# Rebuilding the first stage of a ternary-weight FFN kernel on one Trainium2 core: indices on VectorE, maxima over partitions on TensorE, another order of loads and masks

## The reference, cut to what matters

```python
w = weights[conditions]                        # 128 batches choose among 200 matrices of 64 x 64
c = jnp.einsum('bct,bcd->bdt', x, w)           # x: 128 x 64 x 512, fp32

def ternarize(W, threshold):                   # threshold 0.05
    absW = jnp.abs(W)
    delta = threshold * jnp.max(absW)
    mask = absW > delta
    n = jnp.maximum(jnp.sum(mask), 1)
    alpha = jnp.sum(jnp.where(mask, absW, 0.0)) / n
    return alpha * jnp.sign(W) * mask

h = gelu(c @ ternarize(W1).T + b1)             # W1: 2048 x 512
y = h @ ternarize(W2).T + b2                   # W2: 512 x 2048
scale = jnp.max(jnp.abs(y)) / 7 + 1e-8         # over all of y
out = x + clip(round(y / scale), -7, 7) * scale
```

## Time and profile before

| what | us |
|---|---|
| median of 3 runs | 1045.27 (1043.31 to 1045.33) |
| the profiled execution, its own time | 1043.61 |
| its span, first to last instruction | 1041.8 |
| PE busy in the span | 937.6 |
| DVE / ACT / POOL busy | 648.8 / 553.8 / 157.8 |

### The profile page before, as it was taken

The page is one execution under the profiler, slowest core; times in us unless marked ns, Lnnn a source line. Parts: engine busy times, 40 slices in busy tenths (PEclk is TensorE's granted clock), DMA queues, the critical chain, the costliest instruction groups (busy, mean ns, idle before and its releaser), DMA issues.

```text
span 1041.8 us, 15013 instructions
## 1 busy us (share of the span) xinstructions
PE 937.6 (90%) x5265; PEld 448.1 (43%) x5265; DVE 648.8 (62%) x1007; ACT 553.8 (53%) x710; POOL 157.8 (15%) x213
## 2 busy tenths in 40 slices
PE   0499999999999999999999999999999999999600
PEld 0355444444444444444444444444444444444200
DVE  3599766666666656666665666566666656633492
ACT  3489372727456473828274564638282645535290
POOL 4032303030110203030302102030303021000000
PEclk9899999999999999999999999999999999999855
DMA  6610120301121211203011112121030121105999
GB/s 219 201 44 4 30 63 11 70 21 40 45 45 41 50 40 43 48 10 78 13 40 45 45 40 50 40 50 41 10 81 10 40 47 44 40 0 181 307 386 376
DMA packets 40592, 77.89 MB, mean 75 GB/s; under 512 B 3952, under 2 KB 4352, under 8 KB 40064
## 3 DMA queue, kind: packets, MB, share of 16 engines
q1 hardware_dynamic: 36304, 73.47, 24.3%
q0 software_dynamic: 4096, 3.94, 1.4%
q10 hardware_dynamic: 176, 0.27, 0.1%
HBM read 60.89 MB, written 16.78 MB: 75 GB/s over the span
## 4 chain that ended last, share of the span: by engine, by line
PE 77%; issue 10%; ACT 5%; DVE 3%; POOL 2%; DMA 1%; DVEq 0%; ACTq 0%; SPq 0%; POOLq 0%
PE ps L444 38%; PE ps L456 35%; PE ps L432 3%; ACT y L692 2%; PE ps L474 1%; ACT y L664 1%; POOL ws L356 1%; DVE st L709 1%; DMA yx<-in_x 1%; DVE y L822 0%; DVE y L960 0%; ACT ps L692 0%; DVE wts L819 0%; DMA condb<-in_itok_B 0%; DVE st L768 0%
## 5 line engine op out<-in xcount | busy, mean ns | idle before, releaser
L444 PE MATMUL ps<-yc,wts 128*128 128x512 f16 x2048 | 447.3, 379 | 0.3 <-ACT g L596 0.3
L456 PE MATMUL ps<-wts 128*128 128x512 f16 x1920 | 419.3, 379 | 0.7 <-ACT wts L620 0.7
L444 PEld LDWEIGHTS ps<-yc,wts 128*128 128x128 f16 x2048 | 199.4, 98 | 238.7 <-ACT g L596 0.8
L456 PEld LDWEIGHTS ps<-wts 128*128 128x128 f16 x1920 | 185.8, 98 | 220.4 <-ACT wts L620 0.9
L742 DVE SCALAR_TENSOR_TENSOR wts<-g,st,wts 128x512 f16<-128x512 f32 x256 | 186.4, 749 | 143.0 <-ACT wts L601 141.1
L596 ACT ACTIVATE g<-ps,b1t,st 128x512 f32<-128x512 f32 x256 | 197.8, 773 | 116.7 <-PE ps L444 109.3
L601 ACT ACTIVATE wts<-g,st 128x512 f16<-128x512 f32 x256 | 181.0, 713 | 0.0
L583 ACT ACTIVATE xs<-yx,st 128x2048 f16<-128x2048 f32 x28 | 56.1, 2002 | 145.0 <-DVE st L777 145.0
L378 POOL PARTITION_ALL_REDUCE st<-st x46 | 21.5, 467 | 669.1 <-DVE st L711 413.6
L356 POOL DMA_INDIRECT wg<-in_L_cond_weights,ids x112 | 106.5, 951 | 41.3 <-issue 29.3
L747 DVE SCALAR_TENSOR_TENSOR y<-ps,st,b2b 128x512 f32 (+1 forms) x56 | 41.9, 748 | 78.0 <-PE ps L456 78.0
(11 more groups left out here) (118 smaller groups left out, 377.2 us busy)
## 6 DMA issues: line engine op xcount, KB each, us to landing
yx<-in_x SPq DMA_DIRECT2D x56, 512.0 KB, 6.1
out<-wts SPq DMA_DIRECT2D x12, 512.0 KB, 10.2
y<-in_x SPq DMA_DIRECT2D x5, 1024.0 KB, 10.0
wts<-in_x SPq DMA_DIRECT2D x10, 512.0 KB, 6.0
y<-in_L_ffn_W SPq DMA_DIRECT2D x8, 512.0 KB, 9.0
wts<-in_x SPq DMA_DIRECT2D x4, 1024.0 KB, 5.6
y<-in_L_ffn_W SPq DMA_DIRECT2D x4, 1024.0 KB, 8.0
out<-y SPq DMA_DIRECT2D x4, 1024.0 KB, 12.5
```

The lines of the kernel that those rows point to most:

```text
L444: last = nc.tensor.matmul(psH[:, j % HB, :], T1T[:, k, j * P:(j + 1) * P], csp[:, a, k, :], start=(k == 0 and a == 0), stop=(k == KT - 1 a ...
L456: last = nc.tensor.matmul(psY[:, r % 2, :], hsp[:, a, j, r * P:(r + 1) * P], T2T[:, j, :], start=(j == 0 and a == 0), stop=(j == HT - 1 an ...
```

## The change

Part by part:

- **Indices and constants.** DVE makes the indices (a scan of ones gives 0 to 127, a 32 x 32 transpose brings them to partitions) and the identity matrices; POOL's iota, elementwise instructions and `affine_select` are gone. `condb` is loaded on ACT's queue and `b2b` behind the |W1|.
- **Direct conditioning.** Batches go to two sides of 64 partitions, so a gather fills 128 partitions with two matrices: 4 gathers for a block in place of 8, and no cleared diagonal. The product is `condition_direct`: 16 matmuls of 64 x 128 by 64 x 64 for a half in place of 8 of 128 x 128 by 128 x 128. `x` of blocks 0 and 1 is loaded as four DMAs of 64 partitions (`load_direct`).
- **Maxima by PE.** `wide` spreads a column over 128 columns on DVE, `all_partitions` transposes it on PE in fp32, and DVE reduces the result along the row: for the maximum of `W1`, of the gathered matrices and of `x` of block 0. The scale of `c` of block 0 now comes from the bound 128 x max|x| x max|w| in place of the maximum of `c`, so it is known before `c` is: `high_c0` and `low_c0` read `c` straight from PSUM. POOL's reduction is kept for `b1` (`b1max_all`), behind the gathers of block 0 and ahead of those of block 1.
- **Masks and turns.** All four masks of `W1` stand ahead of its signs, which are cut into 8 pieces; 3 turns in place of 6 stand ahead of `first(0, 0)`, and the tables `AFTER` and `STORES` set where the others go. Two stores follow each gelu at j = 8 to 13 in place of 10 to 15.
- **Loads.** SP issues `W1`, `x` of block 0 and `W2` with no wait between; the half of `x` of block 2 waits for `wide_used`.
- **The count of W2** is PE's: `count2`, 32 matmuls of 512 columns between the last turn of `W2` and `second(0, 0)`, read by DVE after its first `aw2` instruction. It uses the bank `psN`, one of the two banks of `c`, so the conditioning of block 1 stands one `second` later for both halves. ACT's four instructions are gone.

```diff
+    AHEAD, EARLY = 3, 6
+    AFTER = {0: [(1, 3)], 1: [(1, 4)], 2: [(1, 5)], 3: [(1, 6), (1, 7)], **{j: [(1, j + 4)] for j in range(4, 12)}}
+    for j, more in {8: (0,), 9: (1,), 10: (2, 3), 11: (4,), 12: (5, 6), 13: (7, 8), 14: (9, 10), 15: (11,)}.items():
+        AFTER[j] = AFTER.get(j, []) + [(2, n) for n in more]
+    TURNED = 12
+    ORDER = [(1, j) for j in range(AHEAD)] + [piece for j in range(HT) for piece in AFTER[j]] \
+        + [(2, j) for j in range(TURNED, HT)]
+    STORES = [1] * 8 + [2] * 6 + [1] * 2
...
-            sp.dma_start(condb[:, :], cond.rearrange("(a b) -> a b", a=1).to_broadcast([P, B])).then_inc(cond_loaded, 16)
             for c in range(LOADS):
                 sp.dma_start(w1s[:, c * HL:(c + 1) * HL, :], W1_v[:, c * HL:(c + 1) * HL, :]).then_inc(w1_loaded[c], 16)
-            load_direct(0)
-            sp.wait_ge(w_gathered[1], 16 * HALF)
+            load_direct(0, (0, 1))
             for n in range(RT):
                 sp.dma_start(w2s[:, n, :], W2_v[:, n, :]).then_inc(w2_loaded[n], 16)
+            sp.wait_ge(wide_used, 1)
             load_half(0, DIRECT * BB)
-            sp.wait_ge(t1_made, WCH)
+            sp.wait_ge(t1_made, HT // MASKED)
             sp.wait_ge(w1abs_made, LOADS)
-            load_direct(1)
+            load_direct(1, (0, 1))
...
+            def gather_direct(b):
+                for r in range(RT):
+                    nc.gpsimd.indirect_dma_start(
+                        out=wdirect[:, b, r, :], out_offset=None, in_=w_rows[:, :],
+                        in_offset=bass.IndirectOffsetOnAxis(ap=idsd[:, b, r:r + 1], axis=0)).then_inc(wd_gathered[b], 16)
+
+            pool.wait_ge(idx_made, 1)
+            gather_direct(0)
...
-            all_max(max1_part, 1, mx1r, mx1, max1_all)
-            all_max_c(0)
+                all_max(cmax_part, b, mr, ms, cmax_all)
+
+            all_max(b1max_part, 1, mx1r[:, 1:2], mx1[:, 1:2], b1max_all)
...
+            def condition_direct(b, half, bank):
+
+                for k in range(KT):
+                    for j in range(2):
+                        for s in range(2):
+                            side = slice(s * C, (s + 1) * C)
+                            last = nc.tensor.matmul(bank[:, s, k, j * C:(j + 1) * C],
+                                                    xdirect[b][side, 2 * half + j, k * P:(k + 1) * P],
+                                                    wdirect[side, b, 2 * half + j, :], start=True, stop=True)
+                last.then_inc(c_made, 1)
+
+            def all_partitions(q, wide):
+                nc.tensor.transpose(psM[:, q, :], wide, idf).then_inc(wide_turned, 1)
...
+            def count2():
+
+                pe.wait_ge(t2_made, WCH)
+                for n in range(RT):
+                    for c in range(WCH):
+                        hc = slice(c * T, (c + 1) * T)
+                        nc.tensor.matmul(psN, ones[:, :], tern2[:, n, hc], start=(n == 0 and c == 0), stop=False)
+                        last = nc.tensor.matmul(psN, twos[:, :], neg2[:, n, hc], start=False,
+                                                stop=(n == RT - 1 and c == WCH - 1))
+                last.then_inc(n2_counted, 1)
...
-            nc.tensor.transpose(psY[:, 0, 0:HT], b1r[:, :], idf[:, :]).then_inc(b1_turned, 1)
-            condition(0, 0, direct=True)
-            condition(0, 1, direct=True)
-
+            nc.tensor.transpose(psY[:, 0, 0:HT], b1r[:, :], idf[0:HT, 0:HT]).then_inc(b1_turned, 1)
+            pe.wait_ge(wide_made, 1)
+            all_partitions(2, wide1)
             pe.wait_ge(b1_ready, 1)
-            pe.wait_ge(c_copied, 1)
             count1(0)
             count1(1)
-            for j in range(HC):
-                turn1(j)
+            pe.wait_ge(wide_made, 2)
+            all_partitions(1, wide_w)
+            pe.wait_ge(wide_made, 3)
+            all_partitions(0, wide_x)
+            pe.wait_ge(xdirect_loaded, 64)
+            pe.wait_ge(wd_gathered[0], 16 * RT)
+            condition_direct(0, 0, psCd0)
+            condition_direct(0, 1, psCd1)
             count1(2)
             count1(3)
-            for j in range(HC, AHEAD):
+            pe.wait_ge(wide_used, 1)
+            for j in range(AHEAD):
                 turn1(j)
-            pe.wait_ge(c_copied, 2)
+            pe.wait_ge(c0_split, 4)
...
-            condition(1, 0, direct=True)
+                pe.wait_ge(w_stored, ORDER.index((1, j)) + 1)
+                first(0, j, wait_bank=j >= HB, wait_c=False)
+                for weight, n in AFTER[j]:
+                    turn1(n) if weight == 1 else turn2(n)
             for j in range(TURNED, HT):
                 turn2(j)
+            pe.wait_ge(n_read, 1)
+            count2()
             pe.wait_ge(w_stored, 2 * HT)
...
-                condition(i + 1, 1, direct=first_block)
+                if first_block:
+                    pe.wait_ge(xdirect_loaded, 128)
+                    pe.wait_ge(wd_gathered[1], 16 * RT)
+                    pe.wait_ge(n2_read, 1)
+                    condition_direct(1, 0, psCd)
+                else:
+                    condition(i + 1, 1)
                 second(i, 1, wait_bank=not first_block)
+                if first_block:
+                    pe.wait_ge(c_copied, 1)
+                    condition_direct(1, 1, psCd)
...
+            def low_c0(half, s, bank):
+                dve.wait_ge(c0_hi_made, 2 * half + s + 1)
+                nc.vector.scalar_tensor_tensor(out=rows_of_side(csp[:, 1, :, :], half, s), in0=bank[:, s, :, :], scalar=s_c,
+                                               in1=rows_of_side(csp[:, 0, :, :], half, s),
+                                               op0=ALU.mult, op1=ALU.subtract).then_inc(c0_split, 1)
...
+            dve.wait_ge(cond_loaded, 16)
+            link(nc.vector.tensor_scalar(idt, condb[:, :], 0.0, float(S), ALU.is_lt, ALU.mult))
+            link(nc.vector.tensor_tensor(idt, idt, condb[:, :], ALU.add))
+            link(nc.vector.tensor_scalar(idt, idt, 0.0, float(S - 1), ALU.max, ALU.min))
+            link(nc.vector.tensor_scalar(idx[:, :], idt, float(C), pc64, ALU.mult, ALU.add))
...
+            def wide(to, column):
+                nc.vector.tensor_scalar(to, ones_f, column, None, ALU.mult).then_inc(wide_made, 1)
...
-            dve.wait_ge(b1_turned, 1)
-            nc.vector.tensor_copy(b1t[:, :], psY[:, 0, 0:HT]).then_inc(b1_ready, 1)
-            dve.wait_ge(b1_ready, 1)
-            nc.vector.tensor_reduce(mx1[:, 1:2], b1t[:, :], AX.X, ALU.max, apply_absolute_value=True)
-            nc.vector.tensor_reduce(mx1[:, 0:1], wm1, AX.X, ALU.max).then_inc(max1_part, 1)
-            dve.wait_ge(max1_all, 1)
-            nc.vector.tensor_scalar(dl1, mx1r[:, 0:1], THRESHOLD, None, ALU.mult)
-            link(nc.vector.tensor_scalar(nd1, mx1r[:, 0:1], -THRESHOLD, None, ALU.mult))
+            link(nc.vector.tensor_reduce(m1, wm1, AX.X, ALU.max))
+            wide(wide1, m1)
+            dve.wait_ge(wd_gathered[0], 16 * RT)
+            link(nc.vector.tensor_reduce(mxw0[:, 1:2], wdirect[:, 0, :, :], AX.XY, ALU.max, apply_absolute_value=True))
+            wide(wide_w, mxw0[:, 1:2])
+            dve.wait_ge(wide_turned, 1)
+            link(nc.vector.tensor_reduce(m1r, psM[:, 2, :], AX.X, ALU.max))
+            nc.vector.tensor_scalar(dl1, m1r, THRESHOLD, None, ALU.mult)
+            link(nc.vector.tensor_scalar(nd1, m1r, -THRESHOLD, None, ALU.mult))
...
-            for c in range(3):
-                mask_w1(c)
+            mask_w1(0)
+            mask_w1(1)
+            dve.wait_ge(xdirect_loaded, 64)
+            link(nc.vector.tensor_reduce(mxw0[:, 0:1], xdirect[0], AX.XY, ALU.max, apply_absolute_value=True))
+            wide(wide_x, mxw0[:, 0:1])
+            mask_w1(2)
+
+            dve.wait_ge(wide_turned, 3)
+            link(nc.vector.tensor_reduce(mxw0r, psM[:, 0:2, :], AX.X, ALU.max))
+            dve.sem_inc(wide_used, 1)
+            link(nc.vector.tensor_scalar(bxw0, mxw0r, TINY0, None, ALU.max))
+            link(nc.vector.tensor_scalar(bits(pxw0), bits(bxw0), EXPONENT, None, ALU.bitwise_and))
+            link(nc.vector.tensor_scalar(pc, pxw0[:, 0:1], float(2 * C), pxw0[:, 1:2], ALU.mult, ALU.mult))
+            link(nc.vector.reciprocal(rc, pc))
+            nc.vector.tensor_scalar(s_c, rc, TOP, None, ALU.mult).then_inc(cscale_ready, 1)
+            nc.vector.tensor_scalar(mr[:, 1:2], pc, float(2 * KT), None, ALU.mult)
+            mask_w1(3)
+            for c in range(4):
                 positive_w1(c)
-            max_c(0, link)
-            mask_w1(3)
-            scale_c(0, link)
-            positive_w1(3)
-            low_c(0)
+            dve.wait_ge(cscale_ready, 1)
+            low_c0(0, 0, psCd0)
+            low_c0(0, 1, psCd0)
+            positive_w1(4)
+            low_c0(1, 0, psCd1)
+            low_c0(1, 1, psCd1)
+            for c in range(5, HT // MASKED):
+                positive_w1(c)
...
+            dve.wait_ge(b1max_all, 1)
```

(10 more changed lines are left out.)

264 lines of the change are left out of this document (134 added, 130 removed).

## The result

The changed kernel takes 1047.54 us in the median of 13 runs (1045.99 to 1049.85), the kernel before 1044.76 in 13 runs on the same chip (1043.31 to 1045.43): ratio 1.0028, 95% interval 1.002 to 1.0037. It is slower by 0.28%, where the forecast had 1039.8 and 0.8 for faster. The profiled execution has a span of 1044.9 us against 1041.8.

A forecast was written before the change was run, and what follows sets the result against it. PE bounds the fixed-pace loop, DVE the stages ahead of it. Terms -18.9 + 6.8 + 0 + 5.4 + 0.2 + 1.9 = -4.6 us gave 1039.0 from the profile, forecast as 1039.8; own range 1036.5 to 1042, whole range 1034.5 to 1045.

The forecast's parts named there:

- Step 1: First stage: POOL leaves the path and `W1` arrives earlier, so the threshold comes at 19.1 against 38.84, 19.7 us earlier.
- Step 2: First stage, threshold to H: DVE's masks, maxima and copies take 20.0 us against 19.1 before.
- H: The moment from which the first gelu may start: 57.97 us before, forecast 39.1, 18.9 earlier.
- Step 3: Second stage: two stores after each gelu from j = 8 delay `high_h(12)` by 1.0 to 1.5 us; cost +1.0.
- step 4: Before `second(0, 0)`: `count2` adds 6.9 us on PE, little covered; with the doubled stores' cost, +6.8 from H.
- Step 5: Block 1's direct products: both halves on PE's path; 0 if time goes by columns, +1.8 at fp32 pace; 0 taken.
- 6. gap in block 1: Block 1's `first`: later `c` slides the `x` chain, PE waits for a gelu, +5.4; `second(0, 3)` waits too, +0.2.
- step 7: Block 1's `first`: the longer gap drops PE's clock once, 3.8 us at half speed; +1.9, or 0 without a fall.
- The 0.2 us for `second(0, 3)`: Ahead of block 1: PE waits for the bank that a later `store_y` must free; +0.2.
- The kept head start: Rival in block 1: unseen slack in the `x` chain avoids gap and clock fall; -12.1, about 1032 us; chance 0.12.
- Both rivals with a late POOL: First stage: late gathers give 1041.3, or 1042.3 with late `x` (chance 0.14); late POOL code load gives 1047.2 (0.08).
- the slower one: First stage: POOL's code load outlasts the loads, delaying gathers and H by 7.4 us; total +2.8, about 1047.2; chance 0.08.

The follow-up runs named there:

- the full wait: Changed kernel with SP waiting for the last piece of `W1` before issuing `x` of block 0 and `W2`; one run, 1051.82 us.
- the fastest version: Changed kernel with old product places, ACT's count, half a product among the turns, `x` behind `W1`'s sixth piece, old tables: ratio 0.9844 to the kernel before, 1026.97 us.
- both versions with spare products: 112 unused 128-column products while PE awaits `W1`'s maxima, added to the changed kernel with old tables (1044.97 us, 1.0004) and to the fastest version (1028.95 us, 0.9855).

## Why the prediction was wrong

It was wrong by sign: -4.6 us was forecast, and the terms came to +3.7 in the profiles. The steps that failed are 1, 3 and 5.

| step | forecast | measured |
|---|---|---|
| 1. threshold | -19.7 | -16.35 |
| 2. threshold to H | +0.9 | +0.65 |
| 3. second stage, H to the start of `first(0, 15)` | +1.0 | +4.17 |
| 4. from there to `second(0, 0)`, with `count2` | +5.8 | +5.57 |
| 5. direct products | 0 | +2.08 |
| the four `second` beside them | 0 | +0.20 |
| 6. gap in block 1 | +5.6 | +5.55 |
| 7. clock there | +1.9 | +1.83 |

- **Step 1 failed first**, by 3.4 us: "`W1` comes some 0.9 us earlier ... last maximum at 17.4" was 20.8. 2.15 of it is `x`, issued right behind `W1`, which holds up its last pieces; the full wait shows that. The prediction knew of `x` only as something that comes late itself. The other 1.2 is `W1` itself: with `x` out of the way its last piece lands at 17.39, which is 0.35 later than before (17.04) and not 0.9 earlier. Only the first piece is earlier, by 0.2 to 0.4 us. What slows the later ones is open. The index work that moved to DVE cost nothing there: DVE starts its maxima 1.0 us later (8.56 for 7.57), but it has caught up and waits by the seventh piece. POOL, the prediction's doubt at that step, was early.
- **Step 2 was right**: 19.8 us against 20.0.
- **Step 3 failed** by size, 4.2 us for 1.0. It had one mechanism, the doubled stores, priced for j = 12 alone. From H to `first(0, 15)` it is 29.7 us before, 33.9 in the changed kernel, 32.2 in the three profiles with the changed tables in which neither the direct product of block 0 nor `first(0, 0)` was slow, and 29.4 in the fastest version, with the old tables. So 2.7 us are the tables. The other 1.7 are PE's clock at `first(0, 0)` (2.77 us there, at a granted clock of 0.59 and 0.55), a cost for which the prediction has no term: step 7 looks for a fall of the clock only in block 1. PE's wait of 1.46 us for the last ternary part of `W2` lies behind this point and is in the 5.57 of step 4.
- **Step 4 was right in its sum**: 5.8 for 5.6. The count takes the 6.9 us that it was priced at, and 1.3 of them are covered; the prediction took off 1.1 and named only the store wait of 0.69 for it. Taking the count out brings some 5 us, near this net price.
- **Step 5 failed** by a miscount. Before, a half was 8 matmuls of 128 columns; the trace has two records for each fp32 matmul, and the prediction read its 16 records as 16 matmuls. With 8, both theories of that step change places: the columns are as many as before, 1024, so by columns a half costs the same 1.79, and it cost 1.93. The Trainium skill (TensorE: Matmul & The Clock Gate, Weight-path perf modes), read as 128 columns of weights setting the pace of each matmul, would with the right count give 16 x 0.224 = 3.6 us a half. The trace disagrees; the 1.8 more that the prediction drew from it came near only through the miscount.
- **Steps 6 and 7 were right**, in place, chain and size, and putting the products back confirmed them. The 0.2 us for `second(0, 3)` did not come (the last two `second` take 13.82 us with no idle); 0.2 us came instead from the changes between product and `second`. All nine profiles with a gap of 5.2 to 5.9 us have the slow matmuls behind it, 12.4 to 13.2 us for 48.
- **The rivals.** The kept head start fell. Both rivals with a late POOL fell, with POOL's first reduction at 12.91; that the slower one names 1047.2, close to the 1047.54 measured, is chance. The result is slower through sizes that erred the same way (3.4, 3.2 and 2.1) against a forecast gain of 4.6. The range had room for step 5 and a part of step 3, and none for a late `W1`. Its lower end is called the case without a fall of the clock, but 1039.8 less 1.9 is 1037.9, not 1036.5. The gathers of block 1 did not stretch beside the masks: all eight were over by 18.1, ahead of the first mask, so the rule that the prediction brings in for them was not tested. The row of `ternary2` beside the gather at 72.01 is a `scalar_tensor_tensor` with two tensor inputs, and nothing in the trace says that it is in the mode that the rule names.

What stays open: why executions of some kernels with this first stage spread by 7 to 8 us (the changed kernel with the old tables, and both versions with spare products), where the kernel before spreads by 2.8 and 4.4 on the same chips. The profiles show the direct product of block 0 at 3.8 to 7.1 us and `first(0, 0)` at 1.90 to 3.55, so PE's pace there differs between executions, but no run shows that this makes the groups.

## What to carry to other kernels

A gain ahead of a loop of fixed pace is worth what is left of it at the loop's first bound instruction; follow it there through each queue and bank that the edit moved. Ask of a transfer that is issued earlier what it does to those that are ahead of it. The changed first stage was good: with the count and the places of the products put back it gives 0.9%, and with the old tables, a product among the turns and a later `x` 1.6%. The two parts that came with it, a count on the bound engine and a product moved one step later, cost 1.15%, more than all of the 0.9%. And one profile a version is thin where PE's clock differs between executions: the clock in the one profile is not yet a property of the version.

## What the runs showed of the hardware

- Four DMAs of 256 KB to 64 partitions each, behind `W1` in the queue, held the DMA engines busy (share 1.05 to 1.12) at 182 to 249 GB/s, where it was 372 just before. Issued behind `W1`, they delayed its last piece: the last maximum starts at 19.55 with them and at 17.40 without.
- An fp32 matmul of 64 moving columns takes 0.12 us at the granted 2.4 GHz (16 in 1.93) and 0.23 at 1.2 GHz (16 in 3.61, 81.36 to 84.97); one of 128 columns takes 0.22 (8 in 1.79). The weights have 128 columns in both, so it goes by the moving columns.
- Waits of 1.46 and 0.71 us, with short turns between them, brought PE's clock down in some profiles (0.50 from 82 to 84 with the count behind them, 8.65 us for it) and not in the changed kernel's (1.00, 6.91 us). A gap of 5.89 brought it down as well. Gaps of 1.95, 0.32 and 1.86 with long runs of matmuls between them didn't, in one profile.
- POOL's idle of 10 us ahead of its first reduction didn't come in the changed kernel, where four indirect DMAs and four small memsets are all that ran before: the reduction started 0.20 us after the fourth gather, at 12.91. What makes the idle is not shown.
